# A GRU behind a causal convolution on one core: the input product in fp32 for two steps at a time, accumulated in PSUM with bias and recurrence, and the weights loaded ahead of the band of taps

## What is computed

```python
x = x + causal_depthwise_conv(x, cond)         # x: 16 x 256 x 512, 16 taps per channel, cond: 16 x 512
def cell(h, x):                                # h starts as cond; 256 steps, batch 16
    gi = x @ W_ih + b_ih                       # W_ih, W_hh: 512 x 1536
    gh = h @ W_hh + b_hh
    i_r, i_z, i_n = split(gi, 3); h_r, h_z, h_n = split(gh, 3)
    r = sigmoid(i_r + h_r); z = sigmoid(i_z + h_z)
    n = tanh(i_n + r * h_n)
    return (1 - z) * n + z * h
out = x + all_states(x)                        # the state of each step is added to the convolved x
```

## Time and profile before

| what | value |
|---|---|
| median of 3 runs (lowest, highest) | 1139.05 us (1138.99, 1139.3) |
| time of the profiled execution | 1137.38 us |
| its span, first to last instruction | 1135.6 us |
| granted PE clock, mean (1 is 2.4 GHz) | 0.987 |
| PE busy | 1077.6 us (95%) |
| DVE busy | 650.9 us (57%) |
| ACT busy | 414.9 us (37%) |
| POOL busy | 285.4 us (25%) |

### The profile page before, as it was taken

How to read it: one execution, slowest core, us unless ns; L and a number is a source line. 1 busy time by engine, 2 the same in 40 slices (tenths; PEclk the granted TensorE clock), 3 DMA queues, 4 the chain that set the end, 5 groups by cost and what they waited for, 6 DMA issues and landing times.

```text
span 1135.6 us, 50170 instructions
## 1 busy us (share of the span) xinstructions
PE 1077.6 (95%) x20843; PEld 773.5 (68%) x20844; DVE 650.9 (57%) x3213; ACT 414.9 (37%) x1806; POOL 285.4 (25%) x848
## 2 busy tenths in 40 slices
PE   5199999999999999999999999999999999999875
PEld 2187877777777777777777777777777766776543
DVE  1135556565656656565665656566565656666655
ACT  0243334333333333333343333433333343343332
POOL 2332222222222222222222222222222222222221
PEclk9599999999999999999999999999999999999999
DMA  9861614040402204040220404031000000000000
GB/s 161 172 64 21 58 22 40 22 40 3 59 3 41 21 22 40 13 48 4 40 21 21 40 22 40 3 45 17 22 3 21 3 3 22 3 21 3 20 3 21
DMA packets 283013, 35.35 MB, mean 31 GB/s; under 512 B 273312, under 2 KB 282144, under 8 KB 282656
## 3 DMA queue, kind: packets, MB, share of 16 engines
q1 hardware_dynamic: 266128, 30.99, 19.1%
q10 hardware_dynamic: 16656, 1.15, 1.0%
HBM read 23.64 MB, written 8.49 MB: 28 GB/s over the span
## 4 chain that ended last, share of the span: by engine, by line
PE 93%; DVE 3%; ACTq 2%; issue 0%; ACT 0%; DMA 0%; POOLq 0%; DVEq 0%
PE pg L355 59%; PE pgi L320 26%; PE pcv L334 4%; PE pgi L314 2%; ACTq L393 2%; PE pwarm L343 1%; DVE gt L467 1%; DVE hp L504 0%; DVE an L493 0%; ACT rz L432 0%; DMA tz<-taps 0%; DVE arg L478 0%; DVE tz L508 0%; DVE xa L462 0%; DVE gt L472 0%
## 5 line engine op out<-in xcount | busy, mean ns | idle before, releaser
L355 PE MATMUL pg<-whh,hp 128*16 128x192 f32 x16384 | 719.1, 327 | 16.0 <-DVE hp L504 15.8
L355 PEld LDWEIGHTS pg<-whh,hp 128*16 128x16 f32 x16384 | 447.9, 97 | 214.2 <-DVE hp L504 48.8
L289 POOL TENSOR_TENSOR nzh<-rz,hp 128x32 f32<-128x32 f32 x512 | 148.0, 289 | 756.5 <-ACT rz L432 756.5
L467 DVE STREAM_TRANSPOSE gt<-pg 128x128 f32<-128x128 f32 x512 | 156.0, 305 | 291.4 <-PE pg L355 291.4
L432 ACT ACTIVATE rz<-arg 128x64 f32<-128x64 f32 x512 | 133.5, 261 | 490.5 <-DVE arg L478 490.5
L320 PE MATMUL pgi<-xhi,wlo 128*128 128x256 f32 x720 | 226.8, 315 | 0.0
L493 DVE TENSOR_TENSOR_SCAN an<-rz,gates 128x64 f32<-128x64 f32 x512 | 165.4, 323 | 72.5 <-ACT rz L432 45.8
L320 PE MATMUL pgi<-xlo,whi 128*128 128x256 f32 x720 | 202.7, 282 | 0.0
L320 PE MATMUL pgi<-xhi,whi 128*128 128x256 f32 x720 | 202.2, 281 | 0.0
L504 DVE TENSOR_TENSOR_SCAN hp<-zcp,nzh 128x64 f32<-128x64 f32 x512 | 149.4, 292 | 68.0 <-ACT nzh L436 61.9
L320 PEld LDWEIGHTS pgi<-xhi,wlo 128*128 128x128 f32 x720 | 135.5, 188 | 73.8 <-issue 73.8
(11 more groups left out here) (35 smaller groups left out, 238.9 us busy)
## 6 DMA issues: line engine op xcount, KB each, us to landing
xw<-x SPq DMA_DIRECT2D x120, 128.0 KB, 4.4
out<-over SPq DMA_DIRECT2D x10, 512.0 KB, 3.2
over<-w_ih SPq DMA_DIRECT2D x4, 768.0 KB, 7.0
whh<-w_hh SPq DMA_DIRECT2D x1, 3072.0 KB, 16.3
out<-xa SPq DMA_DIRECT2D x5, 512.0 KB, 3.2
tz<-taps ACTq DMA_DIRECT2D x8, 128.0 KB, 4.5
xw<-x SPq DMA_DIRECT2D x8, 64.0 KB, 3.9
out<-xa SPq DMA_DIRECT2D x2, 256.0 KB, 2.8
```

Of the source, the lines that this page charges most:

```text
L289: pool.tensor_tensor(nzh[:, f, :, 1], rz[:, f, 1, :, 1], h_of(t - 1, f), ALU.mult).then_inc(s_zh[f], 1)
L355: m = pe.matmul(pg[f][D * j:D * j + B, 0:3 * CH * D].rearrange("p (g n) -> p g n", g=3), hp[:, t % 2, B * c:B * (c + 1), 1], whh[:, c, :]. ...
L467: dve.transpose(gt[:, f, 0:2 * CH, :].rearrange("p c r -> p (c r)"), pg[f][:, 0:n]).then_inc(s_trz[f], 1)
```

## The change

The input product is no longer made for blocks. `product(m, f, c)` belongs to a pair of steps `m` (steps 2m and 2m+1): the stationary operand is 32 columns of x1 (two steps x 16 batch), the moving one is fp32 W_ih, 128 columns for r and z into the bank `pg[m % 2][f]` and 64 columns for n into a bank `pin[m % 2]`, four column groups `j` each. Half `f = 0` of pair m+1 is made in step 2m, half 1 in step 2m+1, for all four chunks. The high and low parts, the copies to `gates`, and DVE's `args_rz` and `bias_n` are gone. In their place ACT writes the biases to the banks (`seed`, three copies for a pair of steps), every matmul accumulates on what stands there, and DVE transposes `pin` once for a pair (`transpose_in`). The recurrence has 32 stationary columns: h of the step, and zeros at the place of the other step of the pair (`hp` has zero blocks between its chunks for that), so the bank's rows hold both steps. `scan_h` therefore runs over 96 columns in place of 64.

At the start W_ih and W_hh are issued right after `cnd` and a piece `xs` of x, in four parts each, and the band `tz` and all `xw` behind them on the same queue. The first 16 steps are convolved tap by tap: by DVE for three chunks (`first` for steps 0 to 3, `rest` for the others), and by ACT and POOL for the fourth. `ROUNDS` begins at step 5 with the pair of blocks that starts at step 16. x1 is kept whole, so no buffer of it is reused.

```diff
-        ROUNDS = {(1, 0): (2, 9), (1, 1): (11, 13), (2, 0): (15, 23), (2, 1): (27, 36)}
...
-        TURNED = {(1, 0): (9, 11), (1, 1): (13, 15), (2, 0): (23, 27), (2, 1): (36, 40)}
...
+        ROUNDS = {(0, 0): (5, 8), (0, 1): (9, 12)}
+        TURNED = {(0, 0): (8, 10), (0, 1): (12, 14)}
+        for p in range(1, PAIRS):
+            ROUNDS |= {(p, 0): (W2 * p - 16, W2 * p - 3), (p, 1): (W2 * p, W2 * p + 9)}
...
             sp.dma_start(cnd[:, :, :], cond).then_inc(s_cnd, 16)
+            sp.dma_start(xs[:, :, :], x[:, :, 0:TB * B]).then_inc(s_xs, 16)
+            for c in range(C):
+                sp.dma_start(wih[:, c, :, :], w_ih[:, c, :, :]).then_inc(s_wih[c], 16)
+            for c in range(C):
+                sp.dma_start(whh[:, c, :], w_hh[:, c, :]).then_inc(s_whh[c], 16)
+            sp.wait_ge(s_scr, 16)
+            sp.wait_ge(s_band, 1)
+            for l in range(H):
+                for g in range(G):
+                    c, e = l * CH + g // 2, g % 2
+                    sp.dma_start(tz[W2 * g:W2 * (g + 1), l, :, g * K:(g + 1) * K],
+                                 bass.AP(scratch, (e * C + c) * TAPS, [[1, W2], [2 * C * TAPS, P // 2], [1, K]])
+                                 ).then_inc(s_tz, 16)
             load(0, 0)
             load(0, 1)
-            sp.dma_start(bih[:, :], b_ih).then_inc(s_small, 16)
-            sp.dma_start(bhh[:, :], b_hh).then_inc(s_small, 16)
-            for c in range(C):
-                sp.dma_start(wih[:, c, :], w_ih[:, c, :]).then_inc(s_wih[c], 16)
-            sp.dma_start(whh[:, :, :], w_hh).then_inc(s_whh, 16)
             load(1, 0)
             load(1, 1)
...
+            def add_tap(lag):
+
+                a = max(FEW, lag)
+                o = x1[:, C - 1, a * B:TB * B]
+                pool.wait_ge(s_pr, lag + 1)
+                if lag:
+                    pool.wait_ge(s_pa, lag)
+                else:
+                    pool.wait_ge(s_xs, 16)
+                pool.tensor_tensor(o, o if lag else xs[:, C - 1, a * B:TB * B],
+                                   prod[:, lag % PROD, a * B:TB * B], ALU.add).then_inc(s_pa, 1)
+
+            for lag in range(K):
+                add_tap(lag)
+            pool.memset(tz[:, :, :, :], 0.0).then_inc(s_band, 1)
...
-            def product(k, q):
-
-                n = BLOCKS[k] * B
-                m = parts(k)
...
-                    w, xx = ((wlo, xhi), (whi, xlo), (whi, xhi))[part]
-                    ins = pe.matmul(o, w[:, c, u * P:(u + 1) * P], xx[:, k % 2, c, 0:n], **flags)
-                if flags["stop"]:
-                    ins.then_inc(s_gi, 1)
...
+            def product(m, f, c):
+
+                if f == c == 0:
+                    pe.wait_ge(s_seed, 3 * (m + 1))
...
+                        pe.wait_ge(s_x1, 2 * NT * ((2 * m - TB) // W2 + 1))
+                w = wih[:, c, :, :].rearrange("p (g k) (j d) -> p j g k d", g=3, j=J)[:, :, :, f * CH:(f + 1) * CH]
+                xx = x1[:, c, 2 * m * B:(2 * m + 2) * B]
+                for j in range(J):
+                    pe.matmul(pg[m % 2][f][D * j:D * (j + 1), 0:HN], xx, w[:, j, 0:2],
+                              start=False, stop=True, skip_group_check=True)
+                for j in range(J):
+                    i = pe.matmul(pin[m % 2][D * j:D * (j + 1), f * CH * D:(f + 1) * CH * D], xx, w[:, j, 2],
+                                  start=False, stop=True, skip_group_check=True)
+                if f == H - 1 and c == C - 1:
+                    i.then_inc(s_gi, 1)
...
+            def recur(t, f, c):
+
+                for j in range(J):
+                    i = pe.matmul(pg[t // 2 % 2][f][D * j:D * (j + 1), 0:END],
+                                  hp[:, t % 2, 2 * c + 1 - t % 2:2 * c + 3 - t % 2, :, 1].rearrange("p u b -> p (u b)"),
+                                  whh[:, c, :].rearrange("p (g j f n) -> p j f g n", g=3, j=J, f=H)[:, j, f],
+                                  start=False, stop=True, skip_group_check=True)
...
+            pe.wait_ge(s_clear, 1)
+            for q in range(2):
+                for bank in (pg[q][0], pg[q][1], pin[q]):
+                    pe.matmul(bank[:, :], zeros[:, 0:P], zeros[:, :], start=True, stop=True).then_inc(s_bits, 1)
             for _ in range(WARM):
-                pe.matmul(pwarm[:, :], zeros[:, 0:P], zeros, start=True, stop=True).then_inc(s_warm, 1)
...
-                                  whh[:, c, :].rearrange("p (g j f n) -> p j f g n", g=3, j=J, f=H)[:, j, f],
-                                  start=c == 0, stop=c == C - 1)
...
+            for f in range(H):
+                for c in range(C):
+                    if f == 0:
+                        pe.wait_ge(s_wih[c], 16)
+                    product(0, f, c)
...
+                if m + 1 < M2:
+                    for c in range(C):
+                        product(m + 1, t % 2, c)
...
+            def seed(m):
...
+                    act.wait_ge(s_tn[0], 2 * m - 2)
+                    act.wait_ge(s_tn[1], 2 * m - 2)
+                for f in range(H):
+                    act.activation(pg[m % 2][f][:, 0:END], bc[:, f, :], ACT.Copy).then_inc(s_seed, 1)
+                act.activation(pin[m % 2][:, 0:C * D], bcn[:, :], ACT.Copy).then_inc(s_seed, 1)
...
-            def copy(k, u):
-
-                n = BLOCKS[k] * B
...
-                act.activation(o, pgi[v % 2][:, 0:n].rearrange("p (t b) -> p t b", b=B), ACT.Identity,
-                               bias=bsum[:, u:u + 1]).then_inc(s_ev, 1)
...
+            act.wait_ge(s_xs, 16)
+            for lag in range(K):
+                tap_product(lag)
+            act.activation(pre[:, :], cnd[:, 0, :], ACT.Sigmoid)
+            seed(0)
+            seed(1)
...
+                if t % 2 and t + 3 < T:
+                    seed((t + 3) // 2)
...
+            def transpose_in(m):
+                dve.wait_ge(s_gi, m + 1)
+                dve.transpose(gn[:, :, :, :, :, 1].rearrange("p u f c b -> p (f c) u b"),
+                              pin[m % 2][:, 0:C * D]).then_inc(s_tin, 1)
...
-            def args_rz(f):
-
-                dve.wait_ge(s_trz[f], t + 1)
-                dve.tensor_tensor(arg[:, f, :].rearrange("p (c b) -> p c b", b=B), gt[:, f, 0:2 * CH, 0:B],
-                                  gi(k, i, f).rearrange("p (c b) -> p c b", b=B),
-                                  ALU.add).then_inc(s_u[f], 1)
...
-            def bias_n(f):
...
+            def transpose_n(t, f):
+                dve.transpose(gn[:, :, f, :, :, 0].rearrange("p u c b -> p c u b"),
+                              pg[t // 2 % 2][f][:, HN:END]).then_inc(s_tn[f], 1)
...
-                dve.tensor_tensor(gin(k, i, f * HB, HB)[:, :, 0].rearrange("p (c b) -> p c b", c=CH),
-                                  gt[:, f, 2 * CH:, 0:B], bhn[:, f * CH:(f + 1) * CH, :],
-                                  ALU.add).then_inc(s_hn[f], 1)
...
+                a, n = 2 * f * CH + 1, 2 * CH - 1
+                dve.tensor_tensor_scan(hp[:, (t + 1) % 2, a:a + n].rearrange("p c b s -> p (c b s)"),
+                                       zcp[:, f, 0:n].rearrange("p c b s -> p (c b s)"),
+                                       nzh[:, f, 0:n].rearrange("p c b s -> p (c b s)"),
                                        0.0, ALU.mult, ALU.add).then_inc(s_h[f], 1)
...
+            dve.wait_ge(s_xs, 16)
+            for q in range(len(FIRST)):
+                first(q)
+            for q in range(len(REST)):
+                rest(q)
+            dve.wait_ge(s_zero, 4)
+            transpose_in(0)
```

More of the change, by code:

```diff
@@ L32 @@
 K = 16
-R, Z, N = 0, 1, 2
 CB = C * B
@@ L37 @@
 HB = CH * B
-BLOCKS = [8, 8] + [16] * 15
-STARTS = [sum(BLOCKS[:k]) for k in range(len(BLOCKS))]
-NB = len(BLOCKS)
-TB = max(BLOCKS)
-WARM = 60
-WHOLE = 2
-PAIRS = 8
-W2 = 32
-QT = 4
-NT = CH * 4
-TAPS = 48
+G = 2 * CH
+TB = 16
+NB = T // TB
+PAIRS = NB // 2
+W2 = 2 * TB
+QT = 4
+NT = CH * TB // QT
+TAPS = 3 * K
+FEW = 4
+PROD = 4
+WARM = 50
+M2 = T // 2
+HN, END = 2 * CH * D, 3 * CH * D
+STORES = [(n * TB, (n + 1) * TB) for n in range(NB - 1)] + [(T - 16, T - 8), (T - 8, T - 2), (T - 2, T)]
 def build(nc, x, cond, w_ih, w_hh, b_ih, b_hh, out):
-    assert sum(BLOCKS) == T and J * D == P
+    assert J * D == P
     ctx = ExitStack()
@@ L117, in build @@
-        s_xlo = sem("s_xlo")
-        s_whi = sem("s_whi")
-        s_wlo = sem("s_wlo")
+        s_seed = sem("s_seed")
         s_gi = sem("s_gi")
-        s_ev = sem("s_ev")
-        def halves(name):
-            return [sem(f"{name}{f}") for f in range(H)]
+        s_tin = sem("s_tin")
         s_gh = halves("s_gh")
@@ L292, in _ @@
                         add_out(t - 1)
-                for m, steps in SPLIT.items():
-                    for c in range(C):
-                        if t == steps[c]:
-                            xlo_of(m, c)
             add_out(T - 1)
@@ L441, in _, with first @@
-                if k + 1 < NB:
-                    for u in units_done(k + 1, t):
-                        copy(k + 1, u)
```

(47 more changed lines are left out.)

387 lines of the change are left out of this document (129 added, 258 removed).

## The result

The changed kernel takes 1082.68 us (median of 4, 1081.02 to 1083.51) against 1139.17, a ratio of 0.9499 with a 95% interval of 0.9482 to 0.9515. It is 5.0% faster; the forecast was 1065, 6.5% faster. Its profiled execution took 1082.66 us with a span of 1080.9, the one of before 1137.38 and 1135.6. I explain the two spans.

The account below looks back on a forecast made before the run. PE alone was to bound the step: 254 steps 998.2 us, rounds 28.5, last two steps 3.6 and 4.4, wait 3, start 20, end 4.2; span 1061.9, time 1065 us. Forecast band 1056 to 1073; full range 1054 to 1101.

Parts of the forecast that it names:

- rival 3: In the recurrence after a product, changing column widths still costs 0.15 us: 36 us in all, 1101 us; chance 0.1.
- PE's step: PE's work per step without a round: recurrence 2.60, product 1.32, waits and width changes 0.01, together 3.93 us against 4.01.
- the loop: Each step's chain through PE, DVE and ACT for h: 3.55 us, about 0.4 us shorter than PE's 3.93.
- the early start: Before step 0: starting at 20 us in place of 68.3, about 48 us of the 74 us gain.
- Rival 1: Product on PE: short matmuls have a floor, 64-column pairs cost what 128-column ones do, 1174 us; chance 0.05.
- Rival 2: Steps: the loop through DVE and ACT stays the bound at 4.01 us, hiding the rounds, about 1065 us; chance 0.1.
- The first recurrence: Step 0 on PE was to begin at 20 us, after weights, first product, DVE's taps and POOL's work.
- the landing of the weights: W_ih and W_hh, issued from about 1.6 us with 18.4 us for the two, land at about 20 us.
- The taps on DVE: Convolution before step 0: 16 short taps 2 us, 48 of 126 columns on the mean 11.5 us, ending near 18.5.
- The wait for `xw`: PE reaches the first round at the end of step 5, 43.6 us; `xw` lands at 46.5: wait 3 us.
- 254 steps with a product at 3.93: Term of the sum for all steps with a product, each 3.93 us: 998.2 us, rounds counted separately.

## Why the prediction was right, and where its sizes were off

The time of 1082.7 us lies above the 1056 to 1073 of the forecast. The range covers it only because it reached on to rival 3's 1101, and rival 3 didn't come true; that much is luck. The mechanism is right in its three parts, PE's step, the loop and the early start, and one term was left out.

**PE's step: right.** Recurrence 2.60 with 32 stationary columns as with 16. A pair of 128 columns 27.5 ns for 27.3, a step 3.92 for 3.93; the cost of changing widths (rival 3) is gone. Rival 1, the floor, is refuted: eight pairs of 64 columns take 0.11 us, the difference from 30.47 to the next product group at 30.58, 13.8 ns a pair. The Trainium skill's floor of about 25 ns for up to 64 columns (TensorE: Matmul & The Clock Gate, Back-to-back issue gap) does not hold for matmuls in four column groups: 13.8 ns after, at most 15.5 before.

**The loop: right, under PE's step by 0.2 to 0.3 us where I had 0.4.** 3.60 to 3.71 us without the product for 3.55 forecast. Rival 2, that the loop stays the bound, is refuted; with the additions back it binds at 4.09.

**The first recurrence: 22.4 for 20.** The term that failed is the landing of the weights, "about 20". PE waited 3.08 us for W_hh, whose last part was told as landed at 22.2; in other executions with the same order of loads it was 21.0 to 22.4. The sum took 1.6 + 18.4 and so put the 0.5 MB of `xs` ahead at nothing; at the 427 GB/s of 10 to 14 us they are 1.2 us, by an estimate. The taps on DVE were mis-sized more, though the late weights hid it: they ended at 24.6 for 18.5. The 16 short ones took 4.9 us for 2, the 48 others 14.4 for 11.5.'s pitch was too low for them, and they were slower still beside POOL (last section). That is why little is gained by an earlier PE.

**The wait for `xw`: about right in itself** (2.8 us for 3, as the profile's waits have it), in part by luck: PE came to the first round at 47.4 for 43.6, and the landing was as late, 50.4 for 46.5. It is also incomplete. At step 9 PE waits 1.5 us more for DVE's transposes of the first half (`DVE x L395`), since half of them stand in DVE's step 9, behind its gate work, while the rounds of the second half stand in PE's step 9. I had read the two tables and seen only the landing of `xw`.

**The step that failed: "254 steps with a product at 3.93".** Each step was taken at its clean length. The forecast asked what 32 short matmuls cost PE, and not what they cost to be brought there, a term that it put at nothing: one 16 KB packet of instructions every 3.8 us, where before it was one in 6.7. The 12.3 us after step 16, and about 4.9 of the 10.7 before it, are steps late for that. Removing the loads took 7.4 us of the late time and cutting the stores 3.0 more; the kernel before, with the same loads and stores and a packet in 6.7 us, has none. That PE stops for instructions is shown by the place of the gaps, 105 of 105 in four traces at record 191 to 193 of 256, and that the transfers bring it about by these runs. How the transfers hold a packet up, and how far ahead PE holds instructions, was not measured.

## What to carry to other kernels

When a change turns few long matmuls into many short ones, count instructions per microsecond as well as columns, and look at which transfers run beside them: small loads and large stores, issued back to back, delayed PE here by 12 us, and pacing and cutting them gave 11 of 1083 back, together with a later start of the first rounds and 12 more zero matmuls. To see whether PE waits for instructions, count its records up to each gap: here all stood at one place in 256. Where two limits lie within a few hundredths of each other, as PE's work and the loop through DVE did at 4.01 us, work out both for the new kernel, and test each by putting back its part. The new order of the transfers was worth nothing by itself here: price what stands behind the last of them.

## What was not expected of the hardware

PE can wait for its own instructions, and the trace shows it only as "issue". The profile books the packets of instructions on the same 16 transfer engines as data. In the changed kernel the median distance of two packets is 3.79 us, the largest 5.79, and 4.22 on the median ahead of the 27 gaps.

DVE was slower beside POOL. In the case of the weights first, four DVE operations of 16 columns took 7.05 us while POOL's eight subtractions ran from 42.42 to 56.59; in the kernel before, with POOL idle, the same four took 0.64. Each of the four thus took 1.76 us, as long as one of POOL's subtractions (14.17 / 8 = 1.77). At the start of the changed kernel POOL's additions ran from 5.9 to 15.5 us, and taps of 32 columns on DVE took 440 ns on the mean then (L372, near 8 us; two took 240 and two about 640) and 245 near 24 us (L382):

```profile
L372 DVE SCALAR_TENSOR_TENSOR x<-xs,cnd,x 128x32 f32<-128x32 f32 x4 | 1.5, 440 | 0.0
...
L382 DVE SCALAR_TENSOR_TENSOR x<-xs,cnd,x 128x32 f32<-128x32 f32 x3 | 0.6, 245 | 0.0
```

Of the taps of 192 columns those begun between 10.5 and 15.5 us took 439 to 707 ns, and the last four, behind the end of POOL's additions, 404 or 405. The Trainium skill (GPSIMD Engine Reference, section Specifications) has the SBUF interfaces shared with contention for DVE instructions with two SBUF inputs; the two-input taps agree. For the 16-column operations, with one full input and one column, the overlap in time is all that I have.

The clock at the start was not the same in each execution of kernels that begin alike. Step 0 took 5.22 us with a granted clock of 0.50 from 22 to 24 us in one. The same kernel again, and the one with paced loads, had a granted clock of 1.00 through step 0 and took 3.92 us, after the same 3 us of idle PE. Of the eight traces with 50 zero matmuls, four had the lower clock in step 0; of the three with 62, none. Three are too few to show that the 12 more keep it up.
